# Graph attention, linear attention and an int8 layer on one core: query sums read in place, biases moved into the products

## The reference, cut to what matters

```python
xn = layernorm(x)
x = x + gnn(xn, edges) + mix(xn)        # gnn ends in "+ b2"
x = x + ffn(layernorm(x))               # int8 product + bias
# mix, with phi(t) = where(t > 0, t + 1, exp(t)):
q, k, v = split(xn @ W_qkv + b_qkv)     # 12 heads of 64
kv = einsum('hnd,hne->hde', phi(k), v);  z = phi(k).sum(n)
y = phi(q) @ kv / maximum(phi(q) @ z, 1e-6)
out = y @ W_out + b_out
```

## Time and profile before

| | |
|---|---|
| median of 3 runs | 1757.9 us (1757.42 to 1764.39) |
| the profiled execution: its own time | 1760.24 us |
| its span, first to last instruction | 1758.5 us |
| mean granted TensorE clock, as a share of full speed | 0.966 |
| TensorE matmul busy | 1621.5 us (92%) |
| VectorE busy | 1308.4 us (74%) |
| ScalarE busy | 774.4 us (44%) |
| GpSimd busy | 138.1 us (8%) |

### The profile page before, as it was taken

How to read it: one execution, slowest core, us unless ns; L and a number is a source line. 1 busy time by engine, 2 the same in 40 slices (tenths; PEclk the granted TensorE clock), 3 DMA queues, 4 the chain that set the end, 5 groups by cost and what they waited for, 6 DMA issues and landing times.

```text
span 1758.5 us, 34402 instructions
## 1 busy us (share of the span) xinstructions
PE 1621.5 (92%) x10547; PEld 1179.7 (67%) x10548; DVE 1308.4 (74%) x2631; ACT 774.4 (44%) x1021; POOL 138.1 (8%) x245
## 2 busy tenths in 40 slices
PE   4999999987999999889999999989889799999987
PEld 3566667766755666469999999986555455555544
DVE  8698875578749999248899898973664377777785
ACT  4331112222234555168888898863211133333342
POOL 2000000000000000000000000000000033333340
PEclk8999999999899999989999999989999999999999
DMA  5111133323557664541003132132654541011212
GB/s 197 32 58 59 61 73 117 102 79 98 163 157 236 195 194 150 154 128 59 30 30 116 61 110 61 51 98 79 196 171 150 182 154 53 1 53 53 65 55 88
DMA packets 130308, 183.30 MB, mean 104 GB/s; under 512 B 14934, under 2 KB 100088, under 8 KB 130220
## 3 DMA queue, kind: packets, MB, share of 16 engines
q1 hardware_dynamic: 130220, 182.17, 33.4%
HBM read 121.33 MB, written 60.81 MB: 104 GB/s over the span
## 4 chain that ended last, share of the span: by engine, by line
PE 75%; DVE 10%; issue 5%; DMA 3%; ACT 3%; DVEq 2%; POOL 1%; SPq 1%; ACTq 0%; POOLq 0%
PE ps L2044 22%; PE ps L1995 12%; PE ps L2102 7%; PE ps L2101 7%; PE ps L1811 5%; PE ps L1813 4%; PE ps L1812 4%; PE ps L1824 4%; PE ps L1911 2%; PE ps L1885 2%; DVE oh_q L1345 2%; DVE oh_p L1346 1%; PE ps L2113 1%; PE ps L1980 1%; DMA xr_d<-ev 1%
## 5 line engine op out<-in xcount | busy, mean ns | idle before, releaser
L2044 PE MATMUL ps<-xrh,pf 128*128 (+1 forms) x2400 | 399.9, 329 | 11.3 <-DVE pf L1622 11.3
L2044 PEld LDWEIGHTS ps<-xrh,pf 128*128 128x128 f32 x2400 | 393.5, 191 | 17.8 <-issue 15.4
L1811 PE MATMUL ps<-w_hi,xt_hi 128*128 128x384 f16 x600 | 199.6, 333 | 23.9 <-DVE ev L1668 15.4
L1345 DVE TENSOR_SCALAR oh_q<-pat,codeT,neg_w 125x630 f16<-125x630 uint16 x420 | 185.8, 442 | 41.3 <-PE ps L1824 29.7
L1618 DVE SCALAR_TENSOR_TENSOR vb<-vb,tb 128x1260 f32<-128x1260 f32 x120 | 172.9, 1467 | 54.7 <-ACT vb L1119 53.8
L2101 PE MATMUL ps<-x,ph 128*128 (+1 forms) x600 | 196.5, 327 | 16.8 <-POOL pl L921 10.8
L1622 DVE SCALAR_TENSOR_TENSOR pf<-vb,CT 128x1260 f32<-128x1260 f32 x120 | 175.8, 1468 | 35.3 <-PE ps L2044 35.3
L1812 PE MATMUL ps<-w_lo,xt_hi 128*128 128x384 f16 x600 | 199.2, 332 | 0.0
L1813 PE MATMUL ps<-w_hi,xt_lo 128*128 128x384 f16 x600 | 199.1, 332 | 0.0
L2102 PE MATMUL ps<-x,ph 128*128 (+1 forms) x600 | 197.9, 330 | 0.0
L1119 ACT ACTIVATE vb<-qbc,kcol 128x1260 f32<-128x1260 f32 x120 | 161.0, 1345 | 39.5 <-DVE pf L1622 38.1
(11 more groups left out here) (235 smaller groups left out, 2451.1 us busy)
## 6 DMA issues: line engine op xcount, KB each, us to landing
qbc<-tq_d SPq DMA_DIRECT2D x12, 1260.0 KB, 6.6
wst<-in_L_gnn_W SPq DMA_DIRECT2D x60, 192.0 KB, 3.2
xr_d<-ev SPq DMA_DIRECT2D x60, 192.0 KB, 2.0
xrh<-xr_d SPq DMA_DIRECT2D x4, 2880.0 KB, 14.8
x_d<-ev SPq DMA_DIRECT2D x60, 192.0 KB, 2.3
mb_d<-mb SPq DMA_DIRECT2D x30, 310.1 KB
mb<-mb_d SPq DMA_DIRECT2D x30, 310.1 KB
x<-x_d SPq DMA_DIRECT2D x2, 3840.0 KB, 18.9
```

The source lines that it names most:

```text
L1345: dve.tensor_scalar(oh_q[0:ET, u, :], pat[0:ET, :], codes[:, k:k + 1], neg_w[0:ET, ds(w, 1)], ALU.subtract, ALU.is_equal)
L1811: pe.matmul(ps[:, bank, 0:CW], a_hi, hi[:, k, :], start=(k == 0), stop=False)
L2044: mm = pe.matmul(out[b], pf[j][:, b * DB:b * DB + P], x, start=(first and b % 2 == 0), stop=False, skip_group_check=True)
```

## The change

Five things are changed.

- **Query sums.** ScalarE computes relu(-(q + b)) straight from the PSUM bank, with the negated bias as its bias operand, then the exponential; VectorE then writes QF = max(q + (b + 1), q_m), reading the same bank. q_t is gone, q_m has four buffers, and the bank is free when QF is written (q_out; the semaphore q_free is gone). Two small columns, b + 1 and -b, are made by GpSimd (bq_done).
- **Output biases.** b_out + b2 is split into three bfloat16 rows (GpSimd, nine short operations, then a store and a load through DRAM), and each of the 20 output products begins with a matmul of a 3 x 128 block of ones by the three rows. The additions to X, their stores and the wait for them are gone; `load_o` reads x from the input.
- **Groups.** A query block counts four windows: at k = 2, 4, 5 and after k = 5. The window ahead of the y stage is gone, and W_A = 57, so that the y stage counts three windows (blocks 0 to 2) instead of eight.
- **Weight tiles.** Q_TILES is (0, 2, 7, 12, 17, 22, 27): two in the first query block, five in each other, from k = 0 on, each ahead of the group of its step. The y stage has nine tiles, in blocks 0 to 8.
- **Table words.** In the key and value stages VectorE reads the next window's word before it waits for a product instead of after.

```diff
-        q_t = [place(f"q_t{j}", [P, RG], F32, 129024 + 1280 * j) for j in range(2)]
-        q_m = [place(f"q_m{j}", [P, RG], F32, 131584 + 1280 * j) for j in range(2)]
+        q_m = [place(f"q_m{j}", [P, RG], F32, 70656 + 1280 * j) for j in range(NRG)]
...
-        W_A = W_Q + 3 * K6 + 1
-        Q_TILES = (0, 3, 8, 13, 18, 22, 26)
+        W_A = W_Q + 4 * K6
+        Q_TILES = (0, 2, 7, 12, 17, 22, 27)
...
         def step_tile(q, k):
-            t = Q_TILES[q + 1] - K6 + k
-            return range(t, t + 1) if t >= Q_TILES[q] else range(0)
+            t = Q_TILES[q] + (k - 3 if q == 0 else k)
+            return range(t, t + 1) if Q_TILES[q] <= t < Q_TILES[q + 1] else range(0)
...
 # load_o
-            sp.dma_start(oa[n % 4][:, :], acc_d[i * P:(i + 1) * P, c * CW:(c + 1) * CW]).then_inc(oa_in[n % 4], 16)
+            sp.dma_start(oa[n % 4][0:rows, :], x[i * P:i * P + rows, c * CW:(c + 1) * CW]).then_inc(oa_in[n % 4], 16)
...
 # SP, query stage
+            sp.wait_ge(ob_step, 6)
+            sp.dma_start(ob_d.rearrange("j (p c) -> p j c", c=K6), osplit[:, :, :]).then_inc(ob_st, 16)
...
+                if q == 0:
+                    sp.wait_ge(ob_st, 16)
+                    sp.dma_start(orow[:, :], ob_d[:, :]).then_inc(or_in, 16)
             for i in range(NB):
-                sp.wait_ge(xb_done, i + 2)
-                sp.dma_start(acc_d[i * P:(i + 1) * P, :], X[:, i, :]).then_inc(xs_out, 16)
...
 # GpSimd
-            pool.tensor_tensor(bsum[:, :], bsum[:, :], b2_bc0[:, :], ALU.add).then_inc(xb_done, 1)
+            pool.tensor_tensor(ocol[:, :], ocol[:, :], o2col[:, :], ALU.add).then_inc(ob_step, 1)
+            pool.tensor_tensor(bq1[:, :], bq_col[:, :], ones[:, 0:K6], ALU.add)
+            pool.tensor_tensor(nbq[:, :], cst[:, 4:4 + K6], bq_col[:, :], ALU.subtract).then_inc(bq_done, 1)
...
 # ScalarE, query stage
                     for g in range(NRG):
-                        act.wait_ge(q_free, n + 5)
-                        act.wait_ge(q_out, n + 1)
-                        act.activation(q_m[g % 2][:, :], q_t[g % 2][:, :], ACT.Relu, scale=-1.0).then_inc(q_mm, 1)
+                        act.wait_ge(q_done, n + 1)
+                        if n >= NRG:
+                            act.wait_ge(q_out, n - NRG + 1)
+                        act.activation(q_m[g][:, :], ps[:, g, 0:RG], ACT.Relu, bias=nbq[:, 3 * c + fb:3 * c + fb + 1], scale=-1.0).then_inc(q_mm, 1)
...
 # VectorE, key stage (the value stage likewise)
+                        of_w = window(dve, W_K + 2 * ii + j + 1)
                         k_sum(1, NB + 2 * ii + j, j)
-                        count_part(W_K + 2 * ii + j + 1)
+                        one_hots(W_K + 2 * ii + j + 1, *of_w)
...
 # VectorE, query stage
-                    for u in range(2):
-                        count_part(W_Q + 3 * (3 * c + fb) + u + 1)
+                    for u in range(3):
+                        count_part(W_Q + 4 * (3 * c + fb) + u + 1)
                     for g in range(NRG):
-                        dve.wait_ge(q_done, n + 1)
-                        dve.wait_ge(q_out, n + 1)
-                        dve.tensor_scalar(q_t[g % 2][:, :], ps[:, g, 0:RG], sub(bq_col, 3 * c + fb), None, ALU.add).then_inc(q_free, 1)
-                        if g % 2:
-                            for g2 in (g - 1, g):
-                                n2 = (3 * c + fb) * NRG + g2
-                                dve.wait_ge(q_ee, n2 + 1)
-                                dve.scalar_tensor_tensor(sub(QF, 3 * c + fb)[:, g2 * RG:(g2 + 1) * RG], q_t[g2 % 2][:, :], 0.0, q_m[g2 % 2][:, :],
-                                                         ALU.max, ALU.add).then_inc(q_out, 1)
-                    count_part(W_Q + 3 * (3 * c + fb) + 3)
-                    if c == 1:
-                        for u in range(3):
-                            dve.tensor_tensor(sub(X, 3 * fb + u), sub(X, 3 * fb + u), bsum[:, :], ALU.add).then_inc(xb_done, 1)
+                        dve.wait_ge(q_ee, n + 1)
+                        dve.scalar_tensor_tensor(sub(QF, 3 * c + fb)[:, g * RG:(g + 1) * RG], ps[:, g, 0:RG], sub(bq1, 3 * c + fb), q_m[g][:, :],
+                                                 ALU.add, ALU.max).then_inc(q_out, 1)
+                    count_part(W_Q + 4 * (3 * c + fb) + 4)
...
 # TensorE, query stage
                     for k in range(K6):
-                        if k in (2, 4):
-                            count_window(wa + k // 2 - 1, 6, *of_w[k // 2 - 1])
                         for t in step_tile(3 * c + fb, k):
...
                             wq_tile(t)
+                        if k in (2, 4, 5):
+                            count_window(wa + k // 2 - 1 + (k == 5), 6, *of_w[k // 2 - 1 + (k == 5)])
...
-                                if k == 0 and step == 0:
-                                    pe.wait_ge(q_free, n + 1)
+                                if k == 0 and step == 0 and n >= NRG:
+                                    pe.wait_ge(q_out, n - NRG + 1)
...
-                    count_window(wa + 2, 6, *of_w[2])
-            of_w = window(pe, W_A - 1)[1:]
-            count_window(W_A - 1, 6, *of_w)
-            pe.wait_ge(q_out, 2 * 3 * NRG + 2)
+                    count_window(wa + 3, 6, *of_w[3])
+            pe.wait_ge(q_out, 2 * 3 * NRG)
...
 # TensorE, product_steps
+                    if c < C_X and q % PM == 0:
+                        pe.matmul(ps[:, 6 + n % 2, 0:CW], one3[:, :], orow[:, (c - C_O) * CW:(c - C_O + 1) * CW], start=True, stop=False)
```

More of the change, by code:

```diff
@@ L463, in block_tiles @@
         def block_tiles(i):
-            return range(Q_TILES[-1] + i, Q_TILES[-1] + i + 1)
+            return range(Q_TILES[-1] + i, min(Q_TILES[-1] + i + 1, WT_TILES))
         def step_tile(q, k):
-            t = Q_TILES[q + 1] - K6 + k
-            return range(t, t + 1) if t >= Q_TILES[q] else range(0)
-        assert W_A + NB >= NWN and block_tiles(NB - 1)[-1] == WT_TILES - 1
+            t = Q_TILES[q] + (k - 3 if q == 0 else k)
+            return range(t, t + 1) if Q_TILES[q] <= t < Q_TILES[q + 1] else range(0)
+        assert W_A + NB >= NWN and block_tiles(NB - 2)[-1] == WT_TILES - 1
         def store_window(sp, w, stage, u):
@@ L1416, in _ @@
                             n = (2 + c) * NB + i
+                            of_w = window(dve, W_V + 2 * (c * (NB // 2) + ii) + j + 1)
                             dve.wait_ge(g_done, n + 1)
@@ L1894, in _ @@
                 for fb in range(3):
-                    wa = W_Q + 3 * (3 * c + fb)
-                    of_w = [window(pe, wa + u)[1:] for u in range(3)]
+                    wa = W_Q + 4 * (3 * c + fb)
+                    of_w = [window(pe, wa + u)[1:] for u in range(4)]
                     for k in range(K6):
-                        if k in (2, 4):
-                            count_window(wa + k // 2 - 1, 6, *of_w[k // 2 - 1])
                         for t in step_tile(3 * c + fb, k):
@@ L2000, in _ @@
             pe.wait_ge(ct_ev, NWN + 1)
+            pe.wait_ge(or_in, 16)
             product_steps(0, PM)
```

70 lines of the change are left out of this document (41 added, 29 removed).

## The result

The changed kernel takes 1776.09 us (median of 5 runs, 1774.31 to 1780.44) against 1759.43 us of the kernel before (5 runs beside them): a ratio of 1.0096, 95% interval 1.0072 to 1.012. It is slower by 17 us, where I had forecast 1747.7 us and a gain of 10. The profiled execution is one of 1776.09 us, its span 1774.4 us, its mean granted clock 0.953 (before 0.966).

What follows compares the result with a forecast made beforehand. It took TensorE as the bound, busy nine tenths nearly everywhere, with its stalls and half clock as the prize. 0.6 - 5.0 - 7.0 + 1.5 - 0.3 = -10.2 us from 1757.9 gave 1747.7 us, range 1740 to 1757.

Steps and rivals of the forecast that it cites:

- Part 1: Query blocks: without VectorE's copies, blocks two to six need 122.0 us plus 0.5 for gaps: -5.0 us (0 to -5.5).
- C: Query blocks: VectorE pays a 0.93 us pause before every group: +7.5 us, 1755.2 us, chance 0.10.
- the bank wait: Query blocks two to six: TensorE waits 0.35 us per block for the fourth bank to be joined.
- T: Query blocks: the end of a block's last product; the last join was predicted at T + 3.95 us.
- The first query block: The first query block gets one group more and one weight tile less: +0.6 us.
- Parts 2 and 3: Passage to and blocks of y, up to the first output product: 64.9 us against 71.9, -7.0 us (-12 to -2).
- A: Blocks of y: they run at half clock throughout: +4.8 us, 1752.5 us, chance 0.25.
- B: Blocks of y: the clock stays up in all six spacings: -4.8 us, 1742.9 us, chance 0.12.
- Part 4: Output products: twenty bias products of 3 rows at 0.163 us each, net +1.5 us (bounds +3.3 and -0.7).
- Part 5: Key and value blocks: reading the table word ahead of the wait gives -0.3 us (0 to -1.2).
- E: Query blocks: late one-hots keep the stalls and the clock falls in every block: +22.8 us, 1770.5 us, chance 0.05.
- D: Later stages: a transfer or VectorE's masks set the products' pace, so the gain is met again: 1756 us, chance 0.04.

Runs made afterwards that it cites:

- e1_words: The changed kernel, but TensorE reads each group's table word singly, behind the products of k = 1, 3, 4 and 5: 1747.39 us.
- e3_psum: The kernel before with only the new joining: ScalarE and VectorE read the sums from their banks, with four small buffers: 1746.88 us.
- e4: The changed kernel without the twenty bias products, so the first output sums lack the two output biases: 1769.53 us.
- e2_tiles: The changed kernel with four table words still read at the block's top, but the weight tiles placed as before the change: 1754.27 us.
- e9_gap: e1_words with TensorE waiting for the previous block's third join ahead of the first weight tile in query blocks two to six: 1766.27 us.
- e10_rows: e1_words with the bias products on 128 rows in place of 3, the added rows zero, the sums the same: 1744.36 us.
- e7_four: The changed kernel with all four table words read in a row behind the twelve products of k = 1: 1751.29 us.
- e6_two: The changed kernel with two table words read at the block's top, the others behind k = 3 and k = 5: 1763.24 us.

## Why the prediction was wrong

**Part 1, query blocks two to six: the step that failed.** I wrote that "blocks two to six need 48.9 + 20 groups (38.8) + 25 tiles (32.5) + 5 x 0.35 = 122.0 us; I add 0.5 for small gaps". They took 152.3 us. Two terms were missing, and both were put at nothing without a reason. The sum had no term for the table words that TensorE reads at the block's top: the diff turns three into four, and the prediction weighed "more table words per block" for VectorE alone (rival C). The rows of line 448 on TensorE's queue in the kernel before, 0.65 us a word, were there to be read; beneath a group they cost nothing, and I didn't ask whether the fourth group would still cover them. It cost 2.0 us a block. And the clock: the tile was moved to k = 0, where it now stood between that pause and the products. The earlier trace rows had warned that the clock can fall without long idle time; I used that for the blocks of y, and not for the query blocks, where I took clock 1.00. They ran at 0.85, and the half clock cost some 22 us against e1.

With the words read elsewhere (e1_words) the same blocks take 122.9 us (272.4 to 395.3) against my 122.5, the bank wait is 0.36 us against 0.35, and the kernel 1747.39 us against 1747.7. The rest of the working of Part 1 was right, the cost of a join among it: 549 ns mean against 545. VectorE's group I had too dear, 3.6 us against 3.87.

The groups by line of the kernel after, 273 to 424 us, answer to the earlier trace rows:

```profile
L1470 DVE SCALAR_TENSOR_TENSOR QF<-ps,bq,q_m 128x320 f32 x20 | 11.0, 549 | 4.9 <-ACT q_m L1021 4.8
L1019 ACT ACTIVATE q_m<-ps,nbq 128x320 f32<-128x320 f32 x18 | 9.2, 513 | 2.1 <-PE ps L1920 2.1
```

ScalarE's Relu from the bank takes 513 ns instead of 461, and the last join ends at T + 4.3 (306.12 to 310.39) rather than T + 3.95. In e1_words TensorE reaches the fourth bank 0.3 us later than I had it too, at T + 3.9 (T at 297.04, bank asked for at 300.94 and had at 301.37), so that 0.36 us met 0.35 is in part luck: two errors of 0.3 us cancelled. The rule that I cited from the Trainium skill (VectorE: DVE Perf Modes, Rules for kernel authors) leaves both ways open and doesn't say how many readers of a sum are many; with two, e3_psum is 13 us faster without the copies, though it also has four buffers in place of two.

**The first query block** became 2.0 us shorter, not 0.6 longer: it had 3.4 us at half clock in place of 6.8, and its wait for one-hots was 3.0 us in place of 4.1.

**Parts 2 and 3, the passage and the blocks of y: right in the sum, in part by luck.** 64.5 us lie between the last query products and the first output product against 64.9 predicted and 72.0 before; in e1_words 61.8. From the first transposes to the second, 8.0 us pass (434.19 to 442.20) where I had 6.0, and the next two spacings are 5.3 us each where I had 7.3 and 6.0: errors of +2.0 and -2.7 us that nearly cancel. TensorE's rows of the kernel after, in the blocks of y without a group:

```profile
457.23 0.92 PE L1943 MATMUL ps<-ident,yn 128*128 128x128 f32 x6 [0.96 <-DVE yt_lo L1499]
...
461.69 0.92 PE L1943 MATMUL ps<-ident,yn 128*128 128x128 f32 x6 [0.96 <-DVE yt_lo L1499]
...
471.77 1.52 PE L1943 MATMUL ps<-ident,yn 128*128 128x128 f32 x6
...
478.11 1.52 PE L1943 MATMUL ps<-ident,yn 128*128 128x128 f32 x6
```

The spacing is 4.46 us at full clock (I had 4.4) and 6.34 at half clock (6.0). Of the six, three are fast, two slow and one between (5.6); their mean is 5.3, as I had assumed with 5.2. Rivals A and B each describe about half of the blocks.

**Part 4, the biases: mis-sized.** +1.5 us was predicted with +3.3 as upper bound; the stage grew by 4.6 us, by 4.1 through the bias products (e4): in this stretch nineteen of them at 0.36 us are 6.8, less 1.6 and 0.7 of the two waits: 4.5. The step that failed is "I see nothing that makes few rows cheap", which took the spacing of full products, 0.163 us: few rows made it dear, 0.36 us. The nearest row, 371 ns of the earlier trace rows, is a duration, and full products last 330 ns but cost 163; that it is near 0.36 is luck. The trace of the kernel before had the price from start to start, though, around those same products of 6 rows:

```profile
1710.08 0.33 PE L2102 MATMUL ps<-x,pl 128*128 128x385 f16 x1
1710.34 0.37 PE L2111 MATMUL ps<-brow,bone 6*126 6x384 bf16 x1
1710.64 1.19 PE L2113 MATMUL ps<-wf,fqt 128*126 128x384 f16 x6
```

From 1710.08 to 1710.64 are 0.56 us, of which a full product is 0.16: 0.40 us for the one with few rows. Twenty of that should have been the upper bound.

**Part 5** was -0.3 us predicted (at most -1.2) and -1.4 in the two traces, about -1 over all the runs.

**The rivals.** E gave 1770.5 us and half clock in each query block, with a chance of 0.05; it had the size and half of the mechanism, but hung it on a VectorE group of 5.0 us. VectorE fills a group in 3.6 us when nothing holds it (seven pairs, 0.52 us each) and waited 64.7 us for TensorE. Its part was small: TensorE takes the fourth group 3.6 us behind the third (268.14 to 271.76 us), as long as VectorE needs to fill it, so the last one-hots held TensorE's queue by 0.2 us and more, which exposed the reads behind them. C's pause of 0.93 us is 0.49 after the joins. D did not happen: the 17 us lost in the query blocks were kept to the end.

What stays open: how much idle time the clock bears, where between none and 0.7 us ahead of a tile it gives way, and whether the tile or only the place and length of the gap decides. That the one-hots' hold makes the reads late is read from start times (306.12 + 1.5 us after, 326.82 - 0.1 us before, 274.45 + 0.3 us in e2_tiles, the same four reads at the same place without the hold); no run was made for it alone.

## What to carry to other kernels

Count what the engine that sets the pace does between its counted instructions: here a word read into TensorE's registers cost nothing beneath queued matmuls, and up to 0.65 us where the queue had just been held by a semaphore. Put such reads, and any wait, behind dense products rather than between a group and work with few columns: there 1.3 us of idle time cost 3.6 us in each of five blocks (e9_gap). When a loop loses its stalls, ask what the stalls' place had covered.

## What the runs showed of the hardware that was not expected

- A product of 3 rows and 384 columns amid products of 128 rows adds 0.36 us, one of 128 rows 0.16 us (after, e10_rows).
- Four table words take TensorE's queue 2.6 us; behind twelve queued products they idle the matmuls 0.2 us (e7_four), behind a group 0.95 us (e2_tiles), behind a group whose last one-hots were late 2.0 us (after).
- The half clock came with idle time of 0.7 us ahead of a tile with 8 or 2 columns (e6_two, 0.86 in the stage) and stayed away with 0.95 and 0.61 us ahead of query products (e2_tiles, 0.98 in the stage). The Trainium skill, TensorE: Matmul & The Clock Gate, HAM oscillation, warns of long idle gaps only, and a later section (A second HAM failure mode: psum-queue depth-cycling) of frequent small ones between groups of matmuls; of the small ones after, e6_two and e9_gap agree, e2_tiles and e3_psum do not.
- The same query stage of the same instructions took 175.3 and 172.5 us in two executions (after, e4_nobias), at a clock of 0.86 and 0.88.
